# A hybrid layer of gated delta-rule attention and a feed-forward block: output products in other PSUM banks, one product for both heads' sums of squares, and a new order of the steps

## The chip, the cores and the metric

One Trainium2 chip, one of its cores. The time is device microseconds of one launch, the median of the runs. The kernel is float32 throughout; TensorE does a float32 product in two passes, so every product shows as two instructions in the trace.

## What is computed

```python
xn = layernorm(x)                                  # x: 4 batches x 256 tokens x 256
q, k, v, z = split(xn @ w_qkvz.T)                  # 32 heads, 64 wide each
q, k, v = causal_conv(q, k, v, width 4)
q = q / sqrt(sum(q*q) + eps) / 8;  k = k / sqrt(sum(k*k) + eps)
g, beta = -exp(A_log)*softplus(a + dt_bias), sigmoid(b)
for t in range(256):                               # per batch and head, state S is 64x64
    S = S * exp(g_t);  S = S + k_t * ((v_t - k_t.S) * beta_t);  o_t = q_t.S
o = o / sqrt(mean(o*o) + eps) * norm_weight * sigmoid(z)
attention = o @ w_out.T
ffn = hadamard(silu(h @ W_gate.T) * (h @ W_up.T)) @ W_down.T    # h = hadamard(xn), with scales
result = x + attention + ffn
```

## The kernel before

The recursion is done in chunks of 64 tokens: four chunks a sequence, 16 units (4 batches x 4 chunks) for each head. Inside a chunk it is a triangular system, whose inverse is built from 16x16 diagonal blocks; only the state goes from chunk to chunk. Two heads are one pair: head 0 on partitions 0 to 63, head 1 on 64 to 127, and 16 pairs are run one after the other as a software pipeline. One slice of 128 of the feed-forward block's 2 x 1024 rows goes with each pair. Work that stands ahead of the pairs (layer norm, transposes, gates, Hadamard factors) is in `setup`, and is the same in both kernels.

The steps of one pair, by the names that the code uses:
- `proj.0` to `proj.7`: projections of k, k, q, q, v, v, z, z, each 128x512 in one of two PSUM banks (`ring`). ACT does the first tap of the convolution out of the bank (or the tanh for z), DVE three more taps, each an instruction of its own that waits for the last. `ff`: gate and up products, into both `ring` banks.
- `ktr`, `vtr`: transposes of k and v into bank `TR`. `e`: a scan over decay rows, which gives a decay matrix. `stats`: the sums of squares of k and five small operations. `qsq`: q's sums of squares by products with a column of ones; ACT squares q first.
- `gram.0` to `gram.3`: k by k and q by k for one batch each, in the one bank `GR`; DVE multiplies each into `ATP`.
- `bout`, `bin`: SP writes the diagonal blocks to HBM (8 DMAs) and reads them back with another layout. `inv.0` to `inv.2`: DVE inverts all blocks at once, in 17 dependent instructions; ACT makes a transposed copy. `uout`, `uin`: out to HBM, and back in 16 small DMAs.
- `hz.j.H`: four rounds (j) for two halves of the units (H) that make the inverse of the 64x64 system from that of its blocks, products in bank `M[H]`, DVE's subtraction after each round.
- `delta.c`, `state.c`, `ks.c`, `o.t`: the recursion over chunks c in bank `CH`, outputs in bank `Z` for two halves t. `norm.t`: sum of squares of o (ACT, DVE), power -1/2 (POOL). `gated.t`: DVE scales. `turn.t`: transposes, and DVE's product with the z gate.
- `out.0` to `out.3`: the output products (two banks of 256 tokens for each half t), with the feed-forward block's down products in the two of the half `t == m % 2`; DVE adds each to the result `yacc`.

Each engine has its own written-out order, a string that `program` runs once per iteration. The letter before a step says which pair it is for: M this iteration's, A the next, P two ahead, L the one before, K two before. Each engine's iteration may start at another point of the pair's life, so the same letter on two engines need not be the same time. Every engine executes its list strictly in order, and a step first waits for its semaphores. SP's list holds the DMA steps.

Before, one iteration of TensorE is the end of the last pair's recursion and its outputs, then the next pair's first projections between the `hz` rounds, the grams and the start of the recursion:

```python
"""L.state.1 L.o.0 L.ks.2 M.proj.6 L.delta.2 M.vtr.1 L.state.2 M.proj.7 L.ks.3 L.turn.0 L.delta.3 L.o.1 M.ff M.qsq
L.turn.1 L.out.0 L.out.1 L.out.2 L.out.3 A.proj.0 M.hz.0.0 A.proj.1 A.proj.2 A.ktr.0 A.proj.3 M.hz.0.1 M.hz.1.0 A.ktr.1
M.hz.1.1 A.proj.4 M.hz.2.0 M.hz.2.1 A.gram.0 M.hz.3.0 M.hz.3.1 A.gram.1 M.delta.0 A.proj.5 M.state.0 A.gram.2 M.ks.1
A.gram.3 M.delta.1 A.vtr.0"""
```

Of the kernel before, what the change touches and what calls it, by code (L numbers as in the profile page):

```python
# [12 lines left out]
P = 128  # L13
# [5 lines left out]
C = 64  # L19
# [289 lines left out]
def pairs(nc, sem, sb, bank, k, xnT, beta, yacc, xh, wdf, coef, wqkvz, conv, wout, nw, wgu, drows, dblk, dub):  # L309

    with ExitStack() as ctx:
# [60 lines left out]
        TR, GR, M, CH, Z = bank[2], bank[3], [bank[4], bank[5]], bank[6], bank[7]  # L372
        hs = (slice(0, C), slice(C, P))
# [37 lines left out]
        with nc.Block() as block:  # L411
            @block.sync
            def _(sp):
# [78 lines left out]
                program({"load": load, "rload": rload, "fload": fload, "wload": wload, "oload": oload, "bout": bout, "bin": bin_, "uout": uout, "uin": uin}, """A.wload A.uout P.load A.uin A.oload P.rload P.bout P.fload P.bin""")  # L492

            @block.tensor
            def _(pe):
                def proj(m, q, i):

                    if i == 0:
                        pe.wait_ge(w_in, (m + 1) * 16)
                        wait(pe, acc_done, (m - 1) * 4 - 1)  # L500
                        wait(pe, hf_done, m)
                    if i == 1:
                        wait(pe, acc_done, (m - 1) * 4)
                    if i >= 2:
# [115 lines left out]
                def o(m, q, t):  # L620
# [3 lines left out]
                    wait(pe, on_done, m * 2 + t)  # L624
# [22 lines left out]
                def out(m, q, f):  # L647

                    t, j = f // 2, f % 2
                    if f == 0:  # L650
                        pe.wait_ge(wo_done, m + 1)
                        pe.wait_ge(hf_done, min(m + 2, PAIRS))
# [6 lines left out]
                    for b in (2 * j, 2 * j + 1):  # L659
                        dst = ring[j][:, (b % 2) * HID:(b % 2) * HID + HID]  # L660
                        last = nc.tensor.matmul(dst, oT[:, t, b, :], wo[:, q, :], start=True, stop=t != q)  # L661
                        if t == q:
# [4 lines left out]
                         "state": state, "o": o, "turn": turn, "out": out}, """L.state.1 L.o.0 L.ks.2 M.proj.6 L.delta.2 M.vtr.1 L.state.2 M.proj.7 L.ks.3 L.turn.0 L.delta.3 L.o.1 M.ff M.qsq  # L667
                         L.turn.1 L.out.0 L.out.1 L.out.2 L.out.3 A.proj.0 M.hz.0.0 A.proj.1 A.proj.2 A.ktr.0 A.proj.3 M.hz.0.1 M.hz.1.0 A.ktr.1
                         M.hz.1.1 A.proj.4 M.hz.2.0 M.hz.2.1 A.gram.0 M.hz.3.0 M.hz.3.1 A.gram.1 M.delta.0 A.proj.5 M.state.0 A.gram.2 M.ks.1
                         A.gram.3 M.delta.1 A.vtr.0""")  # L670

            @block.scalar
            def _(act):
# [56 lines left out]
                def oload(m, q):  # L730
# [7 lines left out]
                program({"proj": proj, "ff": ff, "dec": dec_, "ktr": ktr, "qsq": qsq, "inv": inv, "delta": delta, "norm": norm, "oload": oload}, """L.proj.6 K.delta.2 L.proj.7 K.delta.3 K.norm.1 L.inv.2 L.qsq L.ff M.proj.0 M.proj.1 M.proj.2 M.proj.3 M.ktr.0 M.ktr.1  # L738
                         M.proj.4 L.delta.0 L.oload M.dec M.proj.5 L.delta.1 L.norm.0""")

            @block.gpsimd
            def _(pool):
# [46 lines left out]
                program({"root": root, "gb": gb, "kd": kd_p, "kqg": kqg_p, "sd": sd, "norm": norm}, """P.gb.0 P.root P.gb.1 P.kd.0 A.sd.1 P.kqg.0 P.kd.1 P.kqg.1 A.sd.2 A.norm.0 A.norm.1""")  # L789

            @block.vector
            def _(dve):
# [135 lines left out]
                def norm(m, q, t):  # L928
# [4 lines left out]
                    if t == 0:  # L933
                        dve.wait_ge(qs_done, m + 1)
# [8 lines left out]
                def turn(m, q, t):  # L943
# [67 lines left out]
```

## Time and profile before

| | |
|---|---|
| time, median of 3 runs | 1015.8 us (1012.44 to 1017.12) |
| the profiled execution | 1015.0 us, span of its instructions 1013.0 us |
| mean granted TensorE clock | 0.957 of full |
| busy: TensorE / DVE / POOL / ACT | 88% / 70% / 26% / 21% |
| chain that ended last, by engine | TensorE 41%, DVE 26%, SP's queue 11%, DMA 10% |
| moved by DMA | 50.93 MB, 47 GB/s of HBM traffic |

The span is from the first to the last instruction. PE stands for TensorE's products, PEld for its weight loads. Busy time of PE is that of overlapping records whose ends are modelled, so the distance between the starts of two groups says more of what one costs. An entry in brackets behind a row of the timeline is idle time of that engine before the row, and what ended it.

### The profile page before, as it was taken

What the parts mean: (1) busy time and instruction counts of PE and PEld (TensorE: products, weight loads), DVE (VectorE), ACT (ScalarE), POOL (GpSimd) and SP (SyncE); (2) the same over time, 40 slices, a digit from 0 to 9 for tenths busy, and PEclk for the clock granted to TensorE, in tenths of its full rate; (3) what the DMA queues carried; (4) which work ended last, traced back from release to release, by engine and by line L of the source; (5) the groups of instructions that cost most, each with busy time, mean ns of one, the idle gap of its engine ahead of it and who ended that gap; (6) DMA issues with size and microseconds to landing.
All of it is one profiled execution on the core that took longest, in us unless ns stands there. A gap on an engine that the chain in (4) does not pass through costs nothing.

```text
span 1013.0 us, 33317 instructions
## 1 busy us (share of the span) xinstructions
PE 895.4 (88%) x14762; PEld 654.0 (65%) x14762; DVE 707.7 (70%) x1272; ACT 213.7 (21%) x384; POOL 262.6 (26%) x186
## 2 busy tenths in 40 slices
PE   1547599999999999999999999999999999999975
PEld 1324376676767676766767676767766676867664
DVE  5755486877777676867777676867777776768622
ACT  1211122222222121222222222222222221212200
POOL 0014051230505050422405050513314050503210
PEclk9879699999999999999999999999999999999978
DMA  4021302122041303032121403031221304031101
GB/s 167 11 63 27 89 6 62 38 63 57 12 91 29 90 8 79 21 66 52 44 59 29 91 12 91 7 72 43 49 55 34 85 13 90 15 83 25 31 10 42
DMA packets 133855, 50.93 MB, mean 50 GB/s; under 512 B 114768, under 2 KB 125264, under 8 KB 133584
## 3 DMA queue, kind: packets, MB, share of 16 engines
q1 hardware_dynamic: 133712, 48.81, 21.1%
q8 instruction: 116, 1.90, 0.8%
q14 instruction: 27, 0.22, 0.1%
HBM read 39.98 MB, written 7.60 MB: 47 GB/s over the span
## 4 chain that ended last, share of the span: by engine, by line
PE 41%; DVE 26%; SPq 11%; DMA 10%; issue 4%; ACT 3%; POOL 0%; POOLq 0%; DVEq 0%; ACTq 0%
PE bank L507 12%; DVE kq L798 8%; PE bank L582 8%; PE bank L563 6%; SPq L461 5%; PE bank L661 4%; DVE E L815 3%; DMA NT<-base_blocks 3%; SPq L485 3%; SPq L487 2%; DVE ATP L843 2%; DMA base_blocks<-ATP 2%; PE bank L580 2%; DMA X<-inverse_blocks 2%; DMA inverse_blocks<-UU 2%
## 5 line engine op out<-in xcount | busy, mean ns | idle before, releaser
L507 PE MATMUL bank<-xnT,wq 128*128 128x512 f32 x512 | 255.0, 624 | 21.8 <-DMA wq<-wqkvz_dram 16.8
L798 DVE SCALAR_TENSOR_TENSOR kq<-bank,cw,kq 128x510 f32<-128x510 f32 (+2 forms) x288 | 214.6, 745 | 58.4 <-ACT kq L685 50.4
L507 PEld LDWEIGHTS bank<-xnT,wq 128*128 128x128 f32 x512 | 89.7, 193 | 105.0 <-issue 68.0
L755 POOL TENSOR_TENSOR gb<-E,stat 128x512 f32<-128x512 f32 x32 | 33.3, 1042 | 447.2 <-issue 428.3
L685 ACT ACTIVATE kq<-bank,cw 128x512 f32<-128x512 f32 x96 | 66.0, 687 | 329.1 <-PE bank L507 329.1
L783 POOL TENSOR_TENSOR ost<-ost,cst 128x8 f32<-128x8 f32 x32 | 52.3, 1634 | 187.2 <-DVE ost L935 187.2
L954 DVE TENSOR_TENSOR yacc<-yacc,bank 128x512 f32<-128x512 f32 x64 | 44.0, 687 | 58.8 <-PE bank L663 40.3
L661 PE MATMUL bank<-wo,oT 128*128 128x256 f32 x256 | 82.0, 442 | 1.7 <-issue 1.6
L563 PE MATMUL bank<-kq 64*64 64x128 f32 x1024 | 69.3, 275 | 10.1 <-DVE ATP L843 10.1
L526 PEld LDWEIGHTS bank<-cst,kq 64*64 64x64 f32 x2048 | 65.9, 135 | 16.6 <-DVE kq L798 13.9
L773 POOL TENSOR_TENSOR kqg<-kq,rows 128x1024 f32<-128x1024 f32 x32 | 75.3, 2354 | 0.0
L526 PE MATMUL bank<-cst,kq 64*64 64x64 f32 x2048 | 72.4, 219 | 2.8 <-ACT ksqj L706 1.8
L843 DVE TENSOR_TENSOR ATP<-bank,gb 128x512 f32<-128x512 f32 x64 | 44.3, 692 | 40.5 <-PE bank L563 38.6
L582 PEld LDWEIGHTS bank<-X,Q 64*64 64x64 f32 x2048 | 62.9, 135 | 11.5 <-DVE X L911 11.4
L563 PEld LDWEIGHTS bank<-kq 64*64 64x64 f32 x1024 | 55.8, 135 | 13.7 <-issue 12.2
L582 PE MATMUL bank<-X,Q 64*64 64x16 f32 (+1 forms) x2048 | 64.6, 212 | 0.0
L661 PEld LDWEIGHTS bank<-wo,oT 128*128 128x128 f32 x256 | 54.3, 221 | 15.0 <-issue 3.8
L723 ACT ACTIVATE d<-bank 128x256 f32<-128x256 f32 x64 | 24.5, 383 | 186.5 <-PE bank L606 186.1
L630 PE MATMUL bank<-d,ATP 64*64 64x64 f32 x1024 | 56.7, 222 | 7.7 <-ACT d L723 7.7
L517 PE MATMUL bank<-xh,wguT 128*128 128x512 f32 x128 | 59.2, 605 | 1.3 <-DMA fc<-coef 1.3
L580 PEld LDWEIGHTS bank<-T,ATP 64*64 64x64 f32 x1024 | 34.1, 141 | 38.9 <-DMA X<-inverse_blocks 26.8
L630 PEld LDWEIGHTS bank<-d,ATP 64*64 64x64 f32 x1024 | 52.7, 135 | 9.9 <-ACT d L723 9.9
(130 smaller groups left out, 1330.8 us busy)
## 6 DMA issues: line engine op xcount, KB each, us to landing
rows<-decay_rows SPq DMA_DIRECT2D x64, 256.0 KB, 4.5
wq<-wqkvz_dram SPq DMA_DIRECT2D x16, 512.0 KB, 3.8
inverse_blocks<-UU SPq DMA_DIRECT2D x16, 256.0 KB, 2.2
base_blocks<-ATP SPq DMA_DIRECT2D x128, 16.0 KB, 1.7
wguT<-wgu_dram SPq DMA_DIRECT2D x8, 256.0 KB, 2.7
NT<-base_blocks SPq DMA_DIRECT2D x16, 128.0 KB, 2.5
U<-inverse_blocks SPq DMA_DIRECT2D x128, 16.0 KB, 2.0
woraw<-wout_dram SPq DMA_DIRECT2D x16, 128.0 KB, 2.3
```

The source lines that it names most:

```text
L507: last = nc.tensor.matmul(ring[i % 2][:], wq[:, q, kc, i // 2, :], xnT[:, kc, (i % 2) * 512:(i % 2) * 512 + 512], start=kc == 0, stop=kc = ...
L517: last = nc.tensor.matmul(ring[j][:], wguT[:, j, kc, :], xh[:, kc].rearrange("p (b t c) -> p b t c", b=B, t=2)[:, :, q, :], start=kc == 0, ...
L526: last = nc.tensor.matmul(TR[hs[h], u * C:u * C + C], kq[hs[h], which, b, w * C:w * C + C], k("eye")[hs[h]], start=True, stop=True)
L563: last = nc.tensor.matmul(GR[hs[h], w * P:w * P + P], kq[hs[h], 0, b, w * C:w * C + C], kq[hs[h], 0:2, b, w * C:w * C + C], start=True, st ...
L580: last = nc.tensor.matmul(dst, ATP[hs[h], q, u, 0, :], T16[hs[h], u, 0:n], start=True, stop=True)
L582: last = nc.tensor.matmul(dst, Q[hs[h], u, :], (U16[hs[h], u, C - n:C] if j == 1 else X[hs[h], q, u, C - n:C]), start=True, stop=True)
L630: last = nc.tensor.matmul(dst, ATP[hs[h], q, u, 1, :], d[hs[h], c % 2, b, :], start=True, stop=c == 0)
L661: last = nc.tensor.matmul(dst, oT[:, t, b, :], wo[:, q, :], start=True, stop=t != q)
L685: nc.scalar.activation(kq[:, i // 2, 2 * (i % 2):2 * (i % 2) + 2, :], split(ring[i % 2][:], 2), ACT.Copy, scale=cw[:, q, i // 2, 3:4]).the ...
L773: nc.gpsimd.tensor_tensor(kqg[:, q, :, half(H)].rearrange("p k u c -> p k (u c)"), src, g, ALU.mult).then_inc(kqg_done, 1)
L798: nc.vector.scalar_tensor_tensor(out=y[:, :, t:S], in0=p[:, :, 0:S - t], scalar=cw[:, q, i // 2, 3 - t:4 - t], in1=y[:, :, t:S], op0=ALU.m ...
L843: nc.vector.tensor_tensor(ATP[:, q, us], GR[:].rearrange("p (u k c) -> p u k c", u=NCH, k=2), gb_[:, us].unsqueeze(2).broadcast_to([P, NCH ...
```

## The change

Three things are changed, in the one function `pairs`.

Banks: the output products go to the banks of the `hz` rounds, `M[1 - j]`, in place of the projections' `ring`. `turn.0` stays in `M[0]`, `turn.1` goes to `Z`, where the recursion's outputs were. The waits follow the banks: the next pair's projections no longer wait for `acc_done` (DVE's additions), the first `hz` round does; `turn.1` no longer waits for `turn.0`'s use; `o.0` waits for the last pair's `turn.1`.

Sums of squares: `qsq` makes one product per unit with all 128 rows and two columns of ones (`hsel`), one column for each head, in place of two products with 64 rows and one column. The result stands on 64 partitions with the heads side by side, so DVE takes it in two reads.

Order: every engine's list is new, and SP's. Pair m's projections now belong to the iteration two before its outputs in all lists.

```diff
+        T2 = [M[0], Z]
@@ SP
-                program({...}, """A.wload A.uout P.load A.uin A.oload P.rload P.bout P.fload P.bin""")
+                program({...}, """K.oload M.load K.uin L.wload L.bout M.fload L.bin M.rload L.uout""")
@@ TensorE: proj
                     if i == 0:
                         pe.wait_ge(w_in, (m + 1) * 16)
-                        wait(pe, acc_done, (m - 1) * 4 - 1)
                         wait(pe, hf_done, m)
-                    if i == 1:
-                        wait(pe, acc_done, (m - 1) * 4)
@@ ktr
-                        wait(pe, qs_done, m)
+                        wait(pe, qs_done, m * 2)
@@ qsq
                     for u in range(UNITS):
-                        for h in range(2):
-                            last = nc.tensor.matmul(TR[hs[h], u:u + 1], kq[hs[h], 1, u // NCH, u % NCH * C:u % NCH * C + C], k("hsel")[hs[h], h:h + 1],
-                                                    start=True, stop=True)
+                        last = nc.tensor.matmul(TR[0:C, 2 * u:2 * u + 2], kq[:, 1, u // NCH, u % NCH * C:u % NCH * C + C], k("hsel"), start=True, stop=True)
@@ hz, j == 0
-                        wait(pe, ogT_done, m * 2)
+                        wait(pe, acc_done, m * 4 - H)
@@ o
-                    wait(pe, on_done, m * 2 + t)
+                    if t:
+                        pe.wait_ge(on_done, m * 2 + t)
+                    else:
+                        wait(pe, ogT_done, m * 2)
@@ turn
-                    if t:
-                        pe.wait_ge(ogT_done, m * 2 + 1)
-                    else:
-                        pe.wait_ge(hz_done, m * 8 + 8)
+                    pe.wait_ge(hz_done, m * 8 + 8)
-                            last = nc.tensor.matmul(M[0][hs[h], i * C:i * C + C], og[hs[h], i, :], k("eye")[hs[h]], start=True, stop=True)
+                            last = nc.tensor.matmul(T2[t][hs[h], i * C:i * C + C], og[hs[h], i, :], k("eye")[hs[h]], start=True, stop=True)
@@ out
-                        pe.wait_ge(hf_done, min(m + 2, PAIRS))
+                        pe.wait_ge(hf_done, m + 1)
-                        dst = ring[j][:, (b % 2) * HID:(b % 2) * HID + HID]
+                        dst = M[1 - j][:, (b % 2) * HID:(b % 2) * HID + HID]
@@ TensorE's order
-    (as quoted above)
+    """M.hz.0.1 M.hz.1.0 M.hz.1.1 A.gram.2 M.hz.2.0 M.hz.2.1 A.gram.3 M.hz.3.0 M.hz.3.1 P.proj.0 M.delta.0 A.vtr.1 M.state.0
+    P.proj.1 M.ks.1 A.qsq M.delta.1 P.proj.2 M.state.1 M.o.0 M.ks.2 P.proj.3 M.delta.2 P.ktr.0 M.state.2 P.proj.4 P.ktr.1
+    M.ks.3 P.gram.0 M.delta.3 M.turn.0 M.o.1 P.proj.5 M.out.0 M.out.1 P.proj.6 M.turn.1 P.vtr.0 P.proj.7 M.out.2 M.out.3
+    P.ff A.hz.0.0 P.gram.1"""
@@ ACT's order
-    """L.proj.6 K.delta.2 L.proj.7 K.delta.3 K.norm.1 L.inv.2 L.qsq L.ff M.proj.0 M.proj.1 M.proj.2 M.proj.3 M.ktr.0 M.ktr.1
-    M.proj.4 L.delta.0 L.oload M.dec M.proj.5 L.delta.1 L.norm.0"""
+    """A.proj.5 M.inv.2 A.ktr.1 A.proj.6 A.proj.7 A.ff A.qsq P.proj.0 M.delta.0 P.proj.1 M.delta.1 A.dec P.proj.2 P.proj.3
+    M.norm.0 M.delta.2 P.ktr.0 M.oload M.delta.3 M.norm.1 P.proj.4"""
@@ POOL's order
-    """P.gb.0 P.root P.gb.1 P.kd.0 A.sd.1 P.kqg.0 P.kd.1 P.kqg.1 A.sd.2 A.norm.0 A.norm.1"""
+    """K.sd.1 K.sd.2 K.norm.0 K.norm.1 M.kqg.0 M.kqg.1 M.gb.0 M.kd.0 M.gb.1 M.root M.kd.1"""
@@ DVE: qsq, norm, turn, out
-                    nc.vector.tensor_scalar(qs[:, q], TR[:, 0:UNITS], EPS, EPS * D, ALU.add, ALU.mult).then_inc(qs_done, 1)
+                    for h in range(2):
+                        nc.vector.tensor_scalar(qs[hs[h], q], TR[0:C, h:2 * UNITS:2], EPS, EPS * D, ALU.add, ALU.mult).then_inc(qs_done, 1)
-                        dve.wait_ge(qs_done, m + 1)
+                        dve.wait_ge(qs_done, m * 2 + 2)
-                    ... in1=split(M[0][:], B) ...
+                    ... in1=split(T2[t][:], B) ...
-                    nc.vector.tensor_tensor(y, y, split(ring[j][:], 2), ALU.add).then_inc(acc_done, 1)
+                    nc.vector.tensor_tensor(y, y, split(M[1 - j][:], 2), ALU.add).then_inc(acc_done, 1)
@@ DVE's order
-    """A.stats M.hz.2.0 M.hz.2.1 A.gram.0 M.hz.3.0 M.hz.3.1 A.gram.1 A.proj.4 M.state.0 A.gram.2 M.ks.1 A.gram.3 A.proj.5
-    M.state.1 M.norm.0 M.ks.2 A.vtr.0 M.gated.0 A.vtr.1 M.state.2 A.inv.0 M.ks.3 A.inv.1 A.inv.2 M.norm.1 M.turn.0
-    M.gated.1 A.ff A.qsq M.turn.1 M.out.0 M.out.1 M.out.2 M.out.3 P.proj.0 A.hz.0.0 P.proj.1 P.proj.2 P.e A.hz.0.1 P.proj.3
-    A.hz.1.0 A.hz.1.1"""
+    """L.out.3 A.gram.0 M.hz.0.0 A.gram.1 M.hz.0.1 M.hz.1.0 A.vtr.0 M.hz.1.1 A.gram.2 M.hz.2.0 A.ff M.hz.2.1 A.gram.3 M.hz.3.0
+    M.hz.3.1 P.proj.0 M.state.0 A.vtr.1 M.ks.1 P.proj.1 A.inv.0 M.state.1 A.qsq P.proj.2 M.ks.2 A.inv.1 M.norm.0 M.state.2
+    P.proj.3 M.ks.3 M.gated.0 A.inv.2 M.turn.0 M.norm.1 P.proj.4 M.gated.1 P.proj.5 M.turn.1 M.out.0 M.out.1 P.e P.stats
+    M.out.2"""
```

## Rows read from the trace of the kernel before

**Rows 1.** The page, busy time of TensorE: busy us (share of the span), instructions.
```profile
PE 895.4 (88%) x14762; PEld 654.0 (65%) x14762; DVE 707.7 (70%) x1272; ACT 213.7 (21%) x384; POOL 262.6 (26%) x186
```

**Rows 2.** Windows of two periods: start:end, length, busy (instructions), clock, DMA, GB/s.
```profile
core 0: us, PE busy (x) PEld busy (x) DVE busy (x) ACT busy (x) POOL busy (x), PEclk, DMA share, GB/s
499.80:555.50 55.70, 52.93 (x915) 38.84 (x912) 41.71 (x77) 12.78 (x23) 15.99 (x11) 1.00 0.24 54
555.50:611.70 56.20, 54.46 (x915) 40.02 (x912) 41.83 (x77) 12.77 (x23) 15.99 (x11) 0.97 0.22 47
```

**Rows 3.** Timeline of TensorE over one period: start, us, what [idle before].
```profile
499.81 3.70 PE L517 MATMUL bank<-xh,wguT 128*128 128x512 f32 x8
503.74 2.03 PE L553 MATMUL bank<-cst,kq 64*64 64x1 f32 x64 [0.23 <-ACT kq L711]
505.63 1.13 PE L644 MATMUL bank<-cst,og 64*64 64x64 f32 x32
506.91 0.67 PE L661 MATMUL bank<-wo,oT 128*128 128x256 f32 x2 [0.15 <-issue]
...
515.07 1.13 PE L580 MATMUL bank<-T,ATP 64*64 64x48 f32 x32 [0.83 <-DMA X<-inverse_blocks]
...
521.24 1.98 PE L507 MATMUL bank<-xnT,wq 128*128 128x512 f32 x4 [0.33 <-DVE kq L798]
...
535.43 1.99 PE L507 MATMUL bank<-xnT,wq 128*128 128x512 f32 x4
537.35 0.68 PE L617 MATMUL bank<-d,kd 64*64 64x64 f32 x16
...
539.79 1.09 PE L563 MATMUL bank<-kq 64*64 64x128 f32 x16 [0.42 <-DVE ATP L843]
...
544.34 0.68 PE L592 MATMUL bank<-St,kqg 64*64 64x64 f32 x16 [0.18 <-DVE St L926]
...
553.46 0.34 PE L630 MATMUL bank<-d,ATP 64*64 64x64 f32 x4 [0.48 <-ACT d L723]
```

**Rows 4.** Timeline of TensorE's weight loads in the setup.
```profile
24.88 3.83 PEld L289 LDWEIGHTS bank<-wbas,xnT 128*64 128x64 f32 x128 [1.04 <-DVE xnT L177]
```

**Rows 5.** Windows around one fall of the clock, and of `hz.2` to `delta.0`.
```profile
447.00:450.40 3.40, 3.16 (x96) 2.80 (x96) 2.25 (x4) 1.12 (x2) 1.56 (x1) 1.00 0.81 240
450.50:453.90 3.40, 3.25 (x13) 2.54 (x9) 1.55 (x4) 0.00 (x0) 0.00 (x0) 0.50 0.36 34
...
529.30:535.40 6.10, 6.10 (x177) 6.02 (x176) 4.34 (x12) 0.69 (x1) 3.85 (x2) 1.00 0.01 3
```

**Rows 6.** Timeline of ACT and DVE: transposed inverse, `e`, last gram, taps, `inv.0`.
```profile
502.10 0.64 ACT L717 ACTIVATE UU<-UU 128x256 f32<-128x256 f32 x1 [1.59 <-DVE UU L897]
...
523.57 2.29 DVE L815 TENSOR_TENSOR_SCAN E<-rows,cst 128x1024 f32<-128x1024 f32 x1
...
540.92 0.69 DVE L843 TENSOR_TENSOR ATP<-bank,gb 128x512 f32<-128x512 f32 x1 [0.95 <-PE bank L563]
541.53 2.30 DVE L798 SCALAR_TENSOR_TENSOR kq<-bank,cw,kq 128x510 f32<-128x510 f32 x3
...
550.39 0.42 DVE L874 TENSOR_TENSOR UU<-NT,cst 128x256 f32<-128x256 f32 x1 [0.84 <-DMA NT<-base_blocks]
```

**Rows 7.** Timeline at the fill and at the tail, TensorE and DVE.
```profile
61.86 5.13 PE L507 MATMUL bank<-xnT,wq 128*128 128x512 f32 x8 [16.82 <-DMA wq<-wqkvz_dram]
...
89.73 0.69 DVE L843 TENSOR_TENSOR ATP<-bank,gb 128x512 f32<-128x512 f32 x1 [1.27 <-PE bank L563]
...
119.29 0.99 PE L580 MATMUL bank<-T,ATP 64*64 64x48 f32 x14 [4.62 <-DMA X<-inverse_blocks]
...
965.27 3.16 PE L580 MATMUL bank<-T,ATP 64*64 64x48 f32 x64 [2.34 <-DMA X<-inverse_blocks]
...
997.06 1.97 PE L644 MATMUL bank<-cst,og 64*64 64x64 f32 x32 [4.05 <-DVE og L941]
```

**Rows 8.** The page's groups: count, busy us, mean ns of one, idle before.
```profile
L685 ACT ACTIVATE kq<-bank,cw 128x512 f32<-128x512 f32 x96 | 66.0, 687 | 329.1 <-PE bank L507 329.1
L783 POOL TENSOR_TENSOR ost<-ost,cst 128x8 f32<-128x8 f32 x32 | 52.3, 1634 | 187.2 <-DVE ost L935 187.2
```

More of the change, by code:

```diff
@@ L491, in _ @@
                     sp.dma_start(nwh[hs[h], :], nw).then_inc(nw_in, 16)
-                program({"load": load, "rload": rload, "fload": fload, "wload": wload, "oload": oload, "bout": bout, "bin": bin_, "uout": uout, "uin": uin}, """A.wload A.uout P.load A.uin A.oload P.rload P.bout P.fload P.bin""")
+                program({"load": load, "rload": rload, "fload": fload, "wload": wload, "oload": oload, "bout": bout, "bin": bin_, "uout": uout, "uin": uin}, """K.oload M.load K.uin L.wload L.bout M.fload L.bin M.rload L.uout""")
             @block.tensor
@@ L666, in _ @@
                 program({"proj": proj, "ff": ff, "ktr": ktr, "vtr": vtr, "qsq": qsq, "gram": gram, "hz": hz, "ks": ks, "delta": delta,
[L667 to L670, printed above, removed]
+                         "state": state, "o": o, "turn": turn, "out": out}, """M.hz.0.1 M.hz.1.0 M.hz.1.1 A.gram.2 M.hz.2.0 M.hz.2.1 A.gram.3 M.hz.3.0 M.hz.3.1 P.proj.0 M.delta.0 A.vtr.1 M.state.0
+                         P.proj.1 M.ks.1 A.qsq M.delta.1 P.proj.2 M.state.1 M.o.0 M.ks.2 P.proj.3 M.delta.2 P.ktr.0 M.state.2 P.proj.4 P.ktr.1
+                         M.ks.3 P.gram.0 M.delta.3 M.turn.0 M.o.1 P.proj.5 M.out.0 M.out.1 P.proj.6 M.turn.1 P.vtr.0 P.proj.7 M.out.2 M.out.3
+                         P.ff A.hz.0.0 P.gram.1""")
             @block.scalar
@@ L737, in _ @@
                 act.wait_ge(nwh_done, 1)
-                program({"proj": proj, "ff": ff, "dec": dec_, "ktr": ktr, "qsq": qsq, "inv": inv, "delta": delta, "norm": norm, "oload": oload}, """L.proj.6 K.delta.2 L.proj.7 K.delta.3 K.norm.1 L.inv.2 L.qsq L.ff M.proj.0 M.proj.1 M.proj.2 M.proj.3 M.ktr.0 M.ktr.1
-                         M.proj.4 L.delta.0 L.oload M.dec M.proj.5 L.delta.1 L.norm.0""")
+                program({"proj": proj, "ff": ff, "dec": dec_, "ktr": ktr, "qsq": qsq, "inv": inv, "delta": delta, "norm": norm, "oload": oload}, """A.proj.5 M.inv.2 A.ktr.1 A.proj.6 A.proj.7 A.ff A.qsq P.proj.0 M.delta.0 P.proj.1 M.delta.1 A.dec P.proj.2 P.proj.3
+                         M.norm.0 M.delta.2 P.ktr.0 M.oload M.delta.3 M.norm.1 P.proj.4""")
             @block.gpsimd
@@ L788, in _ @@
                 nc.gpsimd.memset(Q[:], 0.0).then_inc(preset, 1)
-                program({"root": root, "gb": gb, "kd": kd_p, "kqg": kqg_p, "sd": sd, "norm": norm}, """P.gb.0 P.root P.gb.1 P.kd.0 A.sd.1 P.kqg.0 P.kd.1 P.kqg.1 A.sd.2 A.norm.0 A.norm.1""")
+                program({"root": root, "gb": gb, "kd": kd_p, "kqg": kqg_p, "sd": sd, "norm": norm}, """K.sd.1 K.sd.2 K.norm.0 K.norm.1 M.kqg.0 M.kqg.1 M.gb.0 M.kd.0 M.gb.1 M.root M.kd.1""")
             @block.vector
@@ L946, in turn @@
                     wait(dve, op_ready, (m - 1) * 4 + 2 * t + 2)
-                    nc.vector.scalar_tensor_tensor(out=oT[:, t], in0=zt[:, q, :, t * P:t * P + P], scalar=1.0, in1=split(M[0][:], B),
+                    nc.vector.scalar_tensor_tensor(out=oT[:, t], in0=zt[:, q, :, t * P:t * P + P], scalar=1.0, in1=split(T2[t][:], B),
                                                    op0=ALU.add, op1=ALU.mult).then_inc(ogT_done, 1)
@@ L953, in out @@
                     y = yacc[:].rearrange("p (b t) m -> p b t m", t=2)[:, 2 * j:2 * j + 2, t, :]
-                    nc.vector.tensor_tensor(y, y, split(ring[j][:], 2), ALU.add).then_inc(acc_done, 1)
+                    nc.vector.tensor_tensor(y, y, split(M[1 - j][:], 2), ALU.add).then_inc(acc_done, 1)
                 program({"proj": proj, "ff": ff, "e": e, "stats": stats, "gram": gram, "vtr": vtr, "qsq": qsq, "inv": inv, "hz": hz, "ks": ks,
-                         "state": state, "norm": norm, "gated": gated, "turn": turn, "out": out}, """A.stats M.hz.2.0 M.hz.2.1 A.gram.0 M.hz.3.0 M.hz.3.1 A.gram.1 A.proj.4 M.state.0 A.gram.2 M.ks.1 A.gram.3 A.proj.5
-                         M.state.1 M.norm.0 M.ks.2 A.vtr.0 M.gated.0 A.vtr.1 M.state.2 A.inv.0 M.ks.3 A.inv.1 A.inv.2 M.norm.1 M.turn.0
-                         M.gated.1 A.ff A.qsq M.turn.1 M.out.0 M.out.1 M.out.2 M.out.3 P.proj.0 A.hz.0.0 P.proj.1 P.proj.2 P.e A.hz.0.1 P.proj.3
-                         A.hz.1.0 A.hz.1.1""")
+                         "state": state, "norm": norm, "gated": gated, "turn": turn, "out": out}, """L.out.3 A.gram.0 M.hz.0.0 A.gram.1 M.hz.0.1 M.hz.1.0 A.vtr.0 M.hz.1.1 A.gram.2 M.hz.2.0 A.ff M.hz.2.1 A.gram.3 M.hz.3.0
+                         M.hz.3.1 P.proj.0 M.state.0 A.vtr.1 M.ks.1 P.proj.1 A.inv.0 M.state.1 A.qsq P.proj.2 M.ks.2 A.inv.1 M.norm.0 M.state.2
+                         P.proj.3 M.ks.3 M.gated.0 A.inv.2 M.turn.0 M.norm.1 P.proj.4 M.gated.1 P.proj.5 M.turn.1 M.out.0 M.out.1 P.e P.stats
+                         M.out.2""")
                 dve.wait_ge(acc_done, PAIRS * 4)
```

## The prediction

> **What bounds the kernel now.** I read the page's busy table first: TensorE is busy 88% of the span, far ahead of the rest [rows 1]. That is an average over fill, steady part and tail, so next came the windows of two neighbouring periods, each from one pair's `ff` to the next one's. They last 55.70 and 56.20 us; DVE is busy 41.8 us, ACT 12.8 and POOL 16.0 in either, so only TensorE is near full [rows 2]. The first `hz.0.0` of a pair stands at 119.29 us for pair 0 and at 965.27 for pair 15: 15 periods of 56.4 us, 846 of the 1013 us [rows 7]. The reader is to see that this is a kernel of one period, repeated.
>
> Then the order of TensorE's work in the 55.70 us window, looking for idle time in brackets. Seven rows have it: 0.23 before `qsq` (ACT's squares), 0.15 before `out.0`, 0.83 before `hz.0.0` (the inverse arriving by DMA), 0.33 before a projection (DVE's taps), 0.42 before `gram.3` (the one gram bank), 0.18 and 0.48 in the recursion [rows 3]. They sum to 2.62 us, which leaves 53.1 us of issued products. In the second window the granted clock is 0.97 for a whole period [rows 2]. Short windows show why: 3.4 us at 0.50 while the first output products run, right after `qsq` and `turn.1` [rows 5]. Such a stretch comes in 8 of the 14 periods between pair 1's `ff` and pair 15's and costs half its length, 1.7 us, so about 1.0 us per period. 53.1 + 2.6 + 1.0 is 56.7 against 56.4 measured: the period is accounted for. TensorE's order and its stalls set the time, not another engine.
>
> **q's sums of squares.** Before, 64 instructions (one product is two passes) take 503.74 to 505.63, 1.89 us, 29.5 ns each, two halves of the array side by side. After there are 32, each with 128 rows, 64 weight columns and two moving columns. Nearest row: in the setup, 128 weight loads of just this shape (128x64) take 3.83 us, 29.9 ns each [rows 4]. So 32 take 0.95 us, and 0.94 us per period goes. At the other end a full-height product costs as much as the two half-height ones beside each other (59 ns) and the saving is nothing. I take 0.94, since the row has the same weights; both ends stay. The Trainium skill (TensorE: Matmul & The Clock Gate, LDWEIGHTS) says that a weight load takes its number of columns over 1.2 GHz, whatever the rows: 53 ns for 64 columns, 1.7 us for 32, a saving of 0.2 us. The trace's 29.9 ns disagrees with it; by the page the sum below would be some 11 us longer. DVE's second small read (0.17 us more) lies in DVE's idle time, 14 us a period.
>
> **Banks.** The output products leave `ring`; so the next projections wait for no `acc_done`, and `ff` needn't be consumed before `out.0`. In exchange `hz.j.H` waits for DVE to have added `out.2` and `out.3`. `turn.0` writes `M[0]`, `turn.1` writes `Z`, so neither waits for the other. These cost no work; they are worth what the order makes of them.
>
> **The order.** I followed one period through the five queues with the rows' durations: projection 1.91 us [rows 3], its tap on ACT 0.69, three taps on DVE 2.33, `E` 2.29, DVE's small pieces 0.3 to 0.7 [rows 6, 8], POOL's power 1.63 [rows 8], a group of 32 small products 0.95, 0.2 us for it to drain, 0.04 from one engine to the next. Let T be the end of `o.1`.
> - From T TensorE has `proj.5`, `out.0`, `out.1`, `proj.6`, `turn.1`, `vtr.0`, `proj.7`, `out.2`, `out.3`, `ff`: 16.7 us. Inside it the norm (ACT 0.6, DVE 0.9, POOL 1.65, DVE 0.7) has DVE's taps of `proj.4` beside it and is ready at T+4.9, before `turn.1` at T+6.2 to 7.3. `proj.6` waits for `proj.4`'s taps (T+4.3): no wait where `out.0` and `out.1` carry the feed-forward products (1.73 us each), 0.55 us where they don't (0.87 each). Per period 0.3.
> - DVE meanwhile does `turn.1`, `out.0`, `out.1`, `E`, `stats` (2.1), `out.2`, `out.3`, done at T+15.8. `hz.0.0` is at T+16.7: it doesn't wait for the bank, with 0.9 us to spare.
> - The inverse: ACT's transposed copy stands behind `proj.5`'s tap and starts at T+2.7. Copy, DMA out, 16 DMA issues and landing took from 502.10 to 515.07, 13.0 us [rows 3, 6]; `oload`, now ahead of the load on SP, adds 0.2. T+15.9, 0.8 us ahead of need. The 0.83 us wait of now is hidden.
> - `hz` and `gram` alternate for 10.3 us, with 8 to 9 us of DVE work. `hz.1.1` has 0.15 us to spare, `hz.3.1` 0.4. `vtr.0` on DVE waits for POOL's root, done 3.2 us into the stretch and needed at 4.5.
> - `bout` starts after `gram.3`; `inv.0` can start 9.5 us after that eviction (540.92 to 550.39 now [rows 6]). Its place on DVE comes 10.7 us after it, as two projections' taps stand between. SP's `fload` and `rload` lie in DMA time that nothing waits for.
> - In the recursion `delta.2`'s copy stands behind `proj.3`'s tap and `norm.0` on ACT; `state.2` waits 0.35 us for it. Every other step finds its inputs ready, by 0.1 to 1 us.
>
> So the new period is 53.1 - 0.94 + 0.35 + 0.3 = 52.8. The clock should not fall as now, since `qsq` stands between heavier steps and is half as long.
>
> **The sum.** The fill gets longer: now pair 0's last gram is evicted at 89.73 and `hz.0.0` follows at 119.29. After, all eight projections, `ff` and POOL's root come before that eviction; it ends near 95.5. Inverse blocks +9.5, inversion 12 (it shares DVE with pair 1's taps), copy and DMAs 13: `hz.0.0` near 131. Then 14 full periods, 739, to 870. The period that leads to pair 15's `hz.0.0` has no projections: 9 to the last eviction, 9.5, inversion 11.6, 13.0: 43.5, to 913.5. The tail is now 47.7 us (965.27 to 1013.0); in it `turn.1` waits idle for 4.05 us for the norm [rows 7], and now `out.0` and `out.1` lie in that wait: 44. Span 957.5; the profiled run was 2 us above its span and the median 0.8 above it: 960. With some 2 us for a handoff that I misjudged, **962 us**, 5.3% less.
>
> **Rivals.**
> 1. The full-height product is no cheaper than the pair: +0.94 x 15 = 14 us, **976**. For it: half-height pairs do run side by side. Against: [rows 4].
> 2. The new order has slips of its own. Six handoffs have under 1 us to spare, the old order lost 2.6 us per period in seven. If the new one loses 2.6 instead of 0.6, +2.0 x 15: **991**.
> 3. The change doesn't do what it says: a loop through DVE and the DMAs (inverse late, then `hz`, then `out.3`) takes the idle time's place, 3.5 us per period; the period stays at 56.3 and the time at **1013**. Against it: DVE has 14 us idle, and the chain to `inv.0` has 1.2 us to spare.
> 4. Slower: the clock. The new order puts 10.3 us of 64-row products with 16 to 48 columns together, without a projection. If TensorE ran at 1.2 instead of 2.4 GHz for all of it, each period is 10.3 us longer, **1115**. It decides from 3.5 us per period on, 7 us at half clock; one stretch of 3.4 us per period gives only +1.7 x 15, 987. For it: the clock fell with TensorE busy 3.16 of the last 3.40 us [rows 5]. Against: `hz.2` to `gram.1` are 6.1 us of the same products, at 1.00 [rows 5]. The same page of the Trainium skill (Part 1) has the gate follow how busy TensorE has been, at half or full rate; both levels are in the rows, but the profile's busy time does not foretell the fall, so the page settles nothing here.
>
> **Chances.** Forecast 0.60; rival 1 0.08; rival 2 0.17; rival 3 0.05; rival 4 0.03; 0.07 that the fill, the tail or the handoffs come out better, below 950. The range leaves out rivals 3 and 4, the upper part of rival 2 and the lower part of the last case: 946 to 990. Within 0.5% is about what a measurement of this kernel can't tell from no change. Faster 0.92, same 0.04, slower 0.04.
>
> **What would show it.** Steady distance between `hz.0.0` of neighbouring pairs near 52.8 us. L553's successor: 32 instructions a pair, 0.95 us. No fall of the clock behind it. Idle before the first `hz` product near nothing; 0.35 us before `state.2`; up to 0.55 before `proj.6` in every second pair. First `hz.0.0` near 131, the last near 913. I am wrong if waits on DVE's `X` or `Q`, on `yacc`, or on the inverse's DMA come to over 1 us a period, or if the clock reads 0.50 in the `hz` stretch.

## The result, and the profile after

The changed kernel takes 975.3 us (median of 4 runs, 972.64 to 977.65) against 1014.5 us of the kernel before (median of 4, the three known before and one more): ratio 0.961, with 95% interval 0.957 to 0.965. It is faster by 3.9%; 5.3% was forecast, and the time lies inside the range of 946 to 990.

The page of the kernel after: busy time, and the chain that ended last.

```profile
PE 883.1 (91%) x14250; PEld 652.2 (67%) x14250; DVE 707.4 (73%) x1288; ACT 209.5 (22%) x384; POOL 264.3 (27%) x186
...
PE 77%; DVE 10%; issue 2%; SPq 2%; DMA 1%; POOL 1%; ACT 1%; POOLq 0%; DVEq 0%; ACTq 0%
```

512 instructions fewer on TensorE (16 units x 2 for each of 16 pairs), and the chain is now TensorE for 77% of the span, where it was 41%, with DVE, SP's queue and the DMAs in between. That is what filling the waits looks like.

Two neighbouring periods, from one pair's first `hz.0.0` to the next one's, and a window inside the first, right after the sums of squares (columns as in [rows 2]):

```profile
400.55:454.62 54.07, 53.53 (x881) 39.46 (x880) 41.67 (x78) 12.49 (x23) 17.76 (x14) 0.97 0.23 49
454.62:506.29 51.67, 51.67 (x881) 38.87 (x880) 41.33 (x77) 12.49 (x23) 14.32 (x10) 1.00 0.27 59
420.20:423.20 3.00, 3.00 (x12) 0.98 (x12) 0.96 (x6) 0.52 (x3) 0.00 (x0) 0.55 0.49 122
```

Busy 51.67 of 51.67 us: in every second period TensorE shows no gap at all. The other kind is 2.4 us longer and has the clock at 0.97. From pair 0's `hz.0.0` (137.17) to pair 14's (877.69) it is 14 periods of 52.9 us, 52.8 having been forecast.

The timeline of TensorE in the longer period, at the sums of squares (L550) and at `proj.6` (441.90):

```profile
417.19 2.03 PE L550 MATMUL bank<-cst,kq 128*64 128x2 f32 x32
419.15 0.68 PE L602 MATMUL bank<-Y,X 64*64 64x64 f32 x16
419.76 3.06 PE L505 MATMUL bank<-xnT,wq 128*128 128x512 f32 x4
422.75 1.12 PE L613 MATMUL bank<-d,kd 64*64 64x64 f32 x16
...
441.90 1.98 PE L505 MATMUL bank<-xnT,wq 128*128 128x512 f32 x4 [0.54 <-DVE kq L794]
```

The wait of 0.54 us before `proj.6`, in every second pair, is the one that was forecast at 0.55. But the 32 merged products take 1.96 us (417.19 to 419.15), 61 ns each, about as long as the 64 of before (1.89 us). And the clock falls behind them: the next projection takes 2.99 us in place of 1.91. There are 7 such falls in the steady part, one every second period (209, 315, 420, 526, 632, 738, 844 us), where the kernel before had 8.

### The profile page after: what moved, and what is told of

Its sections match the earlier page's. It is cut to its first block, busy times and chain, and to the rows that moved or that the text cites. A ratio compares the mean times of both kernels' runs of the same rounds, so it can differ in the third digit from the quotient of the medians.

```text
span 970.6 us, 32338 instructions
## 1 busy us (share of the span) xinstructions
PE 883.1 (91%) x14250; PEld 652.2 (67%) x14250; DVE 707.4 (73%) x1288; ACT 209.5 (22%) x384; POOL 264.3 (27%) x186
## 3 DMA queue, kind: packets, MB, share of 16 engines
q8 instruction: 112, 1.84, 0.8%
## 4 chain that ended last, share of the span: by engine, by line
PE 77%; DVE 10%; issue 2%; SPq 2%; DMA 1%; POOL 1%; ACT 1%; POOLq 0%; DVEq 0%; ACTq 0%
PE bank L505 23%; PE bank L578 9%; PE bank L524 6%; PE bank L515 5%; PE bank L559 5%; PE bank L657 4%; PE bank L576 3%; PE bank L602 3%; PE bank L550 3%; DVE kq L794 3%; PE bank L613 3%; PE bank L629 3%; PE bank L588 3%; PE bank L659 3%; PE bank L640 2%
## 5 line engine op out<-in xcount | busy, mean ns | idle before, releaser
L505 PE MATMUL bank<-xnT,wq 128*128 128x512 f32 x512 | 266.5, 646 | 30.3 <-DMA wq<-wqkvz_dram 16.8
L794 DVE SCALAR_TENSOR_TENSOR kq<-bank,cw,kq 128x510 f32<-128x510 f32 (+2 forms) x288 | 214.6, 745 | 58.7 <-ACT kq L681 51.3
L775 POOL TENSOR_TENSOR Sd<-St,dec 128x256 f32<-128x256 f32 x32 | 19.9, 620 | 300.2 <-DVE St L920 195.7
L524 PEld LDWEIGHTS bank<-cst,kq 64*64 64x64 f32 x2048 | 65.5, 136 | 17.6 <-DVE kq L794 13.8
L657 PE MATMUL bank<-wo,oT 128*128 128x256 f32 x256 | 70.2, 387 | 2.9 <-DVE yacc L951 1.5
L657 PEld LDWEIGHTS bank<-wo,oT 128*128 128x128 f32 x256 | 49.3, 194 | 22.1 <-issue 13.3
L629 PE MATMUL bank<-d,ATP 64*64 64x64 f32 x1024 | 59.7, 231 | 0.0
L629 PEld LDWEIGHTS bank<-d,ATP 64*64 64x64 f32 x1024 | 57.0, 144 | 0.0
L908 DVE TENSOR_TENSOR X<-U,bank 128x384 f32<-128x384 f32 (+2 forms) x96 | 40.1, 418 | 22.6 <-PE bank L578 22.6
L631 PE MATMUL bank<-St,kqg 64*64 64x64 f32 x768 | 54.4, 224 | 0.0
```

Source lines behind the costliest of these rows:

```text
L524: last = nc.tensor.matmul(TR[hs[h], u * C:u * C + C], kq[hs[h], which, b, w * C:w * C + C], k("eye")[hs[h]], start=True, stop=True)
L629: last = nc.tensor.matmul(dst, ATP[hs[h], q, u, 1, :], d[hs[h], c % 2, b, :], start=True, stop=c == 0)
L631: last = nc.tensor.matmul(dst, kqg[hs[h], q, 1, u, :], St[hs[h], c % 2, b, :], start=False, stop=True)
L794: nc.vector.scalar_tensor_tensor(out=y[:, :, t:S], in0=p[:, :, 0:S - t], scalar=cw[:, q, i // 2, 3 - t:4 - t], in1=y[:, :, t:S], op0=ALU.m ...
```

## The experiments

All ratios are to the kernel before, run on the same chip in turn. "Falls" are stretches of 3.4 us with the clock at 0.50, counted from 150 us to the `hz.0.0` of pair 14; the mean period is that of the 14 up to there. Both come from the one profiled execution of each kernel. All falls stand behind the sums of squares, but for two of the four in the row "outputs behind `turn.1`".

| kernel | time, us | ratio to before (95%) | falls | mean period |
|---|---|---|---|---|
| changed | 975.3 | 0.961 (0.957 to 0.965) | 7 | 52.9 |
| merged squares alone, old order | 1013.0 | 0.996 (0.994 to 0.999) | 7 | 56.5 |
| banks alone, old order | 1015.5 | 0.998 (0.996 to 1.000) | 6 | 56.2 |
| new order and banks, old squares | 963.8 | 0.948 (0.945 to 0.951) | 1 | 52.1 |
| changed, squares with 32 columns | 960.8 | 0.945 (0.942 to 0.948) | 0 | 52.2 |
| changed, outputs behind `turn.1` | 999.2 | 0.983 (0.980 to 0.986) | 4 | 55.0 |
| changed, squares in alternate halves | 948.8 | 0.933 (0.930 to 0.936) | 0 | 51.4 |
| changed, late `kqg` | 970.3 | 0.954 (0.951 to 0.957) | 7 | 53.0 |
| old squares, late `kqg` | 961.9 | 0.943 (0.940 to 0.946) | 4 | 52.5 |
| alternate halves, late `kqg` | **946.1** | 0.930 (0.927 to 0.932) | 0 | 51.3 |
| that, `ktr.1` before `proj.6` | 953.0 | 0.935 (0.933 to 0.938) | 0 | 51.9 |

**Merged squares alone.** The diff's `qsq` and DVE's two reads, put into the kernel before.

> The kernel before with one part of the change alone: q's sums of squares by one full-height product per unit, and DVE's two reads; banks and order as before. Theory 1 (a full-height product whose result goes to 64 partitions costs as much as the two half-height ones side by side): the step still takes 1.9 to 2.0 us, the clock still falls behind it, the time is that of before, 1014 us within 3. Rival (the product costs 29.9 ns as the setup's weight loads, and something in the new order made it slow): the step takes 0.95 us and the time is 995 to 1002 us.

1013.0 us. The timeline of TensorE:

```profile
450.78 2.03 PE L552 MATMUL bank<-cst,kq 128*64 128x2 f32 x32 [0.23 <-ACT kq L709]
452.73 1.15 PE L642 MATMUL bank<-cst,og 64*64 64x64 f32 x32
```

1.95 us for 32 instructions in the old order too, for 1.89 of before. Theory 1 holds: the merge saves no time on TensorE. Why the whole is 0.4% shorter, with an interval that just leaves out 1, no run shows.

**The old squares in the new order.**

```diff
-                        last = nc.tensor.matmul(TR[0:C, 2 * u:2 * u + 2], kq[:, 1, ...], k("hsel"), ...)
+                        for h in range(2):
+                            last = nc.tensor.matmul(TR[hs[h], u:u + 1], kq[hs[h], 1, ...], k("hsel")[hs[h], h:h + 1], ...)
```

> The changed kernel with the old two half-height products per unit and DVE's one read; new banks and new order. Theory 1: the step takes 1.9 us, the time stays at 975 us within 3, so all of the gain is the order and the banks. Rival (merging is worth something that the step's own length does not show, such as fewer instructions in TensorE's queue): 980 to 990 us.

963.8 us: faster than the changed kernel, which neither expectation had. The step takes 1.84 us, but the clock falls once, at 418 us, and only the period with that fall is 53.9 us long. So order and banks together bring 5.2%, and the merge takes 1.3 points of it back. Six falls fewer at 1.6 us, and a step shorter by 0.12 us in 16 pairs, are 11.5 us of estimate, and the times differ by 11.5. The falls vary between executions, though: one of the six took 969.5 us, at a mean clock of 0.952 for 0.959 to 0.962 in the others.

**Alternate halves.**

```diff
-                        last = nc.tensor.matmul(TR[0:C, 2 * u:2 * u + 2], kq[:, 1, ...], k("hsel"), ...)
+                        last = nc.tensor.matmul(TR[hs[u % 2], u // 2 * 2:u // 2 * 2 + 2], kq[:, 1, ...], k("hsel"), ...)
...
                     for h in range(2):
+                        for r in range(2):
+                            nc.vector.tensor_scalar(qs[hs[h], q, r:UNITS:2], TR[hs[r], h:UNITS:2], EPS, EPS * D, ALU.add, ALU.mult).then_inc(qs_done, 1)
```

> The changed kernel with the full-height products of even units written to PSUM partitions 0 to 63 and those of odd units to 64 to 127, and DVE's reads four in place of two; the same values. Theory 1 says that neighbouring products run side by side when they go to different halves of the partitions, as those of the setup do: the step takes 0.95 to 1.0 us in place of 1.96, and the clock no longer falls behind it; period 51.7 and 54.1 become about 50.7 and 51.3, the time 945 to 952 us. Rival (the setup's 29.9 ns come from its other shape, 32 moving columns from another tile): the step stays at 1.96 us, the time at 975.

948.8 us, in the range. The timeline of TensorE, and the windows of two periods:

```profile
460.26 1.10 PE L550 MATMUL bank<-cst,kq 128*64 128x2 f32 x32
461.29 0.68 PE L602 MATMUL bank<-Y,X 64*64 64x64 f32 x16
```

```profile
391.77:443.62 51.85, 50.94 (x880) 37.79 (x881) 41.75 (x79) 11.94 (x23) 16.76 (x12) 1.00 0.23 51
443.62:494.43 50.81, 50.60 (x880) 37.87 (x880) 41.66 (x79) 12.39 (x23) 14.11 (x10) 1.00 0.27 60
```

The longer of the two is usually 51.63 us. The same instructions on the same operands take 1.03 us where they took 1.96; only the half of the partitions that the result goes to has changed, and with it DVE's reads, four for two. The setup's products, from which the forecast took 29.9 ns, alternate between the halves too, after every four instructions (`bank[4][h * C:h * C + C]`). The Trainium skill says as much (TensorE: Matmul & The Clock Gate, Part 3: small products run concurrently when their outputs lie in different column groups, which the output's start partition picks); this pair of runs agrees. With the shorter period the inverse has become nearly the limit: before four of the fourteen steady `hz.0.0` it lands only 0.04 us ahead, once after a wait of 1.18 us.

```profile
391.77 1.14 PE L576 MATMUL bank<-T,ATP 64*64 64x48 f32 x32 [1.18 <-DMA X<-inverse_blocks]
```

**32 columns.** The second operand is `hsel` and the 30 constants behind it: more work in the array, the same number of products.

```diff
-                        last = nc.tensor.matmul(TR[0:C, 2 * u:2 * u + 2], kq[:, 1, ...], k("hsel"), ...)
+                        last = nc.tensor.matmul(TR[0:C, 32 * u:32 * u + 32], kq[:, 1, ...], k("hsel32"), ...)
...
-                        nc.vector.tensor_scalar(qs[hs[h], q], TR[0:C, h:2 * UNITS:2], ...)
+                        nc.vector.tensor_scalar(qs[hs[h], q], TR[0:C, h:32 * UNITS:32], ...)
```

> The changed kernel with 32 moving columns in place of 2 in each product of the sums of squares; the first two are the columns of ones, the other 30 results are read by nobody. Theory 3 (every second period is 2.4 us longer mostly because the clock falls after the sums of squares, whose products use the array little): the step still takes about 2 us, the clock stays at 1.00 in the steady part, the longer periods go from 54.1 to about 52.3, the time is 960 to 965 us. Rival (the longer periods come from handoffs that differ between even and odd pairs): 975 us or more.

960.8 us, in the range; its windows and the step:

```profile
400.81:453.32 52.51, 51.97 (x881) 38.80 (x881) 41.43 (x77) 11.90 (x23) 17.07 (x13) 1.00 0.23 51
453.32:505.02 51.70, 51.70 (x882) 38.88 (x881) 41.35 (x77) 12.51 (x23) 14.34 (x10) 1.00 0.27 59
```

```profile
417.45 2.05 PE L551 MATMUL bank<-cst,kq 128*64 128x32 f32 x32
419.44 0.68 PE L603 MATMUL bank<-Y,X 64*64 64x64 f32 x16
```

Sixteen times the columns in 1.99 us in place of 1.96, and no fall. The longer period goes from 54.07 to 52.51; the 0.8 us left over the shorter one are the wait before `proj.6` and what goes with it. Theory 3 holds: without the falls the 14 periods take 731.2 us in place of 740.5. That is 9.3 us; the medians differ by 14.5, and where the rest comes from the traces don't say (this one is of the slowest of six executions, the changed kernel's of the fastest of four). All six executions have a mean clock of 0.965 to 0.969, all four of the changed kernel 0.948 to 0.954, so the falls aren't missing by chance.

**Banks alone.** All of the diff's lines on banks and waits, none on squares and order.

> The kernel before with the new banks and their waits alone; squares and order as before. Theory 2 (the banks pay nothing by themselves, they only allow the new order): 1014 us within 4, the waits for DVE's taps, the gram bank, the inverse and ACT's copies all still there. Rival (the waits on acc_done and hf_done were a hidden part of the period): up to 1.4 us per period less, 993 to 1000 us.

1015.5 us: theory 2, no gain by itself. The waits of [rows 3] are still there. The one for the gram bank (us in all, times, longest us) is the same 10.1 us in both kernels:

```profile
PE bank L561 <- DVE ATP L841: 10.1, 17, 2.8
```

**Outputs behind turn.1.**

```diff
-P.proj.5 M.out.0 M.out.1 P.proj.6 M.turn.1 P.vtr.0
+P.proj.5 P.proj.6 M.turn.1 M.out.0 M.out.1 P.vtr.0
```

> The changed kernel with the first two output products moved in TensorE's list from between proj.5 and proj.6 to behind turn.1; all else as changed. Theory 4 (the new order pays because work that is ready stands in front of each wait, here the output products in front of the taps of proj.4): proj.6 waits 2.4 us in every period in place of 0.54 in every second one, 2.1 us more per period, 1005 to 1009 us. Rival (the queue is bound by issued work alone, and such a wait is made up elsewhere in the period): 975 us within 4.

999.2 us, 24 us more in place of 32. The wait came as computed, in every period:

```profile
456.43 1.98 PE L505 MATMUL bank<-xnT,wq 128*128 128x512 f32 x4 [2.27 <-DVE kq L794]
```

The mean period is 55.0 us, the 2.1 more than 52.9 that were forecast. The steady periods are 54.55 us, 2.9 more than 51.67 and 2.1 more than 52.48, the changed kernel's longer period without a fall (shown below). The clock fell only 4 times, all before 275 us, and not once in the eleven periods of 54.55 us. Two of the four (at 212.5 and 270.6 us) stand behind the sums of squares, the other two (178.4 and 236.4) behind the new wait itself:

```profile
233.00:236.40 3.40, 1.38 (x3) 0.68 (x4) 3.26 (x6) 1.97 (x4) 3.40 (x2) 1.00 0.47 127
236.40:239.80 3.40, 3.40 (x35) 2.28 (x34) 1.82 (x3) 0.00 (x0) 2.69 (x2) 0.50 0.58 160
```

That the time rose by 24 and not by 32 us is not in these periods: they took 29.6 us more, while the last period and the tail are 3.1 us shorter in the profiled executions. Theory 4 holds.

**Late kqg.** Twice: on the alternate halves, and on the changed kernel.

```diff
-K.sd.1 K.sd.2 K.norm.0 K.norm.1 M.kqg.0 M.kqg.1 M.gb.0 M.kd.0 M.gb.1 M.root M.kd.1
+K.sd.1 K.sd.2 K.norm.0 K.norm.1 M.gb.0 M.kd.0 M.gb.1 M.root M.kd.1 M.kqg.0 M.kqg.1
```

> The kernel with alternate halves (948.8 us), with POOL's two long products kqg moved in its list from ahead of gb to behind the last kd. Theory 5 (in the fill, two of DVE's inversion steps take 2.0 and 1.3 us more while a kqg runs on POOL, and that delays the first hz round): no DVE inversion step over 1.1 us, first hz.0.0 3 us earlier, steady period as before, 944 to 947 us. Rival (the fill waits for something else, or kqg now delays hz or the squares in every period): 949 us or more.

> The changed kernel with POOL's kqg moved behind the last kd and nothing else; squares merged as changed. Theory 5: first hz.0.0 3 us earlier, about 971 us. For the clock: if merged products in this order draw it down in themselves, 7 or so falls again in the steady part and periods of 51.7 and 54.1 in turn; if the falls were the luck of where the period fell, a fill that is 3 us shorter gives another number, down to 1 as with the two half-height products, and 961 us.

946.1 and 970.3 us. The reason to try it is in the changed kernel's fill, where DVE and POOL stand so:

```profile
111.79 2.61 DVE L881 TENSOR_TENSOR prod<-UU 128x64 f32<-128x64 f32 x2
119.99 2.39 DVE L893 TENSOR_TENSOR prod<-UU,part 128x512 f32<-128x512 f32 x1
...
427.38 0.56 DVE L881 TENSOR_TENSOR prod<-UU 128x64 f32<-128x64 f32 x2
436.30 1.09 DVE L893 TENSOR_TENSOR prod<-UU,part 128x512 f32<-128x512 f32 x1
```

```profile
111.89 2.38 POOL L769 TENSOR_TENSOR kqg<-kq,rows 128x1024 f32<-128x1024 f32 x1 [17.65 <-DVE kq L794]
118.25 3.19 POOL L769 TENSOR_TENSOR kqg<-kq,rows 128x1024 f32<-128x1024 f32 x1 [3.98 <-DVE kq L794]
```

With `kqg` elsewhere the two steps take their steady 0.57 and 1.08 us:

```profile
113.64 0.57 DVE L881 TENSOR_TENSOR prod<-UU 128x64 f32<-128x64 f32 x2
...
119.80 1.08 DVE L893 TENSOR_TENSOR prod<-UU,part 128x512 f32<-128x512 f32 x1
```

So the stretching is POOL's doing. It was worth less than I expected. The last piece of the inverse landed 1.4 us earlier in the changed kernel (134.16 for 135.60) and 2.9 on the halves (131.12 for 134.03), and the first `hz.0.0` came 1.4 us earlier (135.77 for 137.17) and 1.7 on the halves, not 3. In this fill `hz.0.0` waits last for something else: it follows `ff` without a gap, 1.6 us after the inverse has landed, and `ff` waits for ACT's tanh of `proj.7`. In the changed kernel:

```profile
133.57 3.67 PE L515 MATMUL bank<-xh,wguT 128*128 128x512 f32 x8 [0.78 <-ACT zt L685]
137.17 1.13 PE L576 MATMUL bank<-T,ATP 64*64 64x48 f32 x32
```

The gains in time are hardly clear of the noise. On the halves it is 2.7 us, and the intervals of the ratios overlap; on the changed kernel it is 5.0 us, with intervals that just don't, but the two profiled spans differ by only 1.3 us. The other half of the question, the clock, came out as 7 falls again, but not at the same places. The first three stand in every second period, as before; then one came in the other kind, and the rest kept to that one. So the two kinds of period can be seen with and without a fall:

```profile
665.86:719.16 53.30, 53.30 (x881) 39.37 (x881) 40.99 (x77) 12.49 (x23) 13.96 (x10) 0.97 0.26 57
719.16:771.64 52.48, 51.94 (x882) 38.80 (x881) 41.95 (x78) 12.49 (x23) 18.13 (x14) 1.00 0.23 50
```

53.30 with a fall for 51.67 without, 54.08 for 52.48: a fall costs 1.6 us in either.

**The old squares with late kqg**, the diff of two runs above together.

> The changed kernel with the two half-height products per unit and POOL's kqg behind the last kd: the same as the one with late kqg that fell 7 times in the steady part, but for the squares. If the shape of the merged product draws the clock down in this order: at most 2 falls in the steady part, 957 to 961 us. Rival (the single fall with half-height products was luck): 5 or more falls, 967 to 971 us.

961.9 us and 4 falls: between the two expectations. Two shapes, two positions: merged 7 and 7, in pairs 1 and 4. The trace with 4 is that of the slowest of six executions (965.1 us). Over all of them the mean clock is 0.948 to 0.956 in the ten executions with merged products, 0.952 to 0.964 in the twelve with pairs. The pairs draw the clock down less often in this order, but not never, and by a number that varies.

**ktr.1 in front of the wait.** The idea was to win the 0.54 us before `proj.6` in the fastest kernel.

```diff
-P.proj.4 P.ktr.1 M.ks.3 ... M.out.0 M.out.1 P.proj.6 M.turn.1
+P.proj.4 M.ks.3 ... M.out.0 M.out.1 P.ktr.1 P.proj.6 M.turn.1
```

> The kernel with alternate halves and late kqg (946.1 us), with the transposes ktr.1 moved in TensorE's list from behind proj.4 to in front of proj.6, so that 0.95 us of ready work stands before the wait for proj.4's taps. Theory 4 (ready work in front of a wait pays its length, up to the wait): the periods of 51.63 and 50.81 us in turn become 50.8 to 51.0 in all, 939 to 942 us. Rival (ktr.1 was itself cover for ks.3, or its copies on ACT now hold up vtr.0 or the next projections): 946 us or more.

953.0 us, 7 us slower. Nearly all periods are now alike, but at 51.84, not 50.8. The wait before `proj.6` is gone; two others, before `delta.2` and `delta.3`, stand in every period. The first was there before, but only in every second one; the second is new:

```profile
420.02 0.68 PE L602 MATMUL bank<-Y,X 64*64 64x64 f32 x16 [0.21 <-DVE Y L914]
...
425.89 0.68 PE L602 MATMUL bank<-Y,X 64*64 64x64 f32 x16 [0.39 <-DVE Y L914]
```

`ktr.1` had stood in front of `ks.3` and `gram.0`. Without it TensorE comes to `delta.3` before DVE has made `Y`, which stands in DVE's list behind the taps of `proj.3`. The rival was right in number, and nearly in cause: the cover was for `delta.3`, two steps on. The kernel with alternate halves and late `kqg` stays the fastest: 7% under the one before, 3% under the changed one. A piece of ready work covers one wait or another; moving it paid for one and lost the other.

## Why the prediction was right, and where it was off

**The bound and the mechanism: right.** TensorE's order and its stalls set the time, and filling them was the gain. Banks alone bring nothing measurable, and moving one pair of outputs out of its place costs 2.1 to 2.9 us a period. That the order needs the banks is argued from the waits in the diff; no run had the new order with the old banks. Rivals 2, 3 and 4 did not come. The new order's own slips in the steady part were the 0.54 us of every second period and little else. The inverse was in time, though with less room than the 0.8 us forecast in some periods: it landed 0.04 to 1.2 us before `hz.0.0`, and at the short end was itself waited for (294.79, 612.13 us). The clock read 1.00 in the stretch of `hz` and `gram`:

```profile
457.40:464.80 7.40, 7.40 (x230) 7.39 (x226) 5.84 (x11) 1.06 (x1) 0.61 (x1) 1.00 0.01 3
```

**q's sums of squares: the term was mis-sized.** 0.94 us per period was taken off; the merged step took 1.96 us where it had been 1.89. The step that failed is the choice of the row: [rows 4] has the same weights but a result that alternates between the halves of the partitions, which the row doesn't show and the code does. Rival 1's premise was true. That its 976 us came within 1 us of the time is luck: its 14 us stand for a longer period, and the period was as forecast; 12 of the 13 us missing were outside the steady periods (below). The 53 ns of the Trainium skill's page (TensorE: Matmul & The Clock Gate, LDWEIGHTS) lay nearer to the 61 ns measured than the row did, but the load's own length is not what decides: in alternate halves the same 64-column loads follow every 32 ns.

**"The clock should not fall as now": wrong.** It fell 7 times in 14 periods, some 0.8 us per period. The reason given, heavier steps around a shorter one, had the length from the same row.

**The period came out right, 52.9 for 52.8, by luck: errors cancelled.** The two points above make the forecast 1.8 us too short. On the other side, the 53.1 us of "issued products" held waits that have no bracket. In the timeline before:

```profile
524.13 1.10 PE L582 MATMUL bank<-U,Q 64*64 64x48 f32 x32
525.07 1.15 PE L526 MATMUL bank<-cst,kq 64*64 64x64 f32 x32
526.37 1.13 PE L582 MATMUL bank<-U,Q 64*64 64x48 f32 x32
```

From the first start to the second it is 0.94 us for 32 small products, from the second to the third 1.30 for as many: 0.36 us of waiting for DVE's `Q` that the modelled end of the row before covers. The brackets of [rows 3] hide such pieces too. From `turn.1` to `out.0` it is 1.28 us (505.63 to 506.91), 1.13 without the bracket; after, `turn.1` takes 0.98 (497.21 to 498.19). The clean period of after is 51.67 us with the same products, so by this difference 1.5 us of the 53.1 were such waits, and the new order removed them too. The wait before `state.2`, forecast at 0.35, shows only as 0.14 us of that kind (`ktr.0` takes 1.09 us from start to start, for 0.95).

**The ends: 12 of the 13 us.** By the profiled span (970.6 against 957.5): the first `hz.0.0` at 137.2 for 131, 14 periods 740.5 for 739, the short period 45.1 for 43.5, the tail 47.8 for 44. In the fill the last gram was evicted at 95.9 and `inv.0` began at 105.9, as computed (95.5 and 105); then the inversion took 17 us, not 12, with POOL's `kqg` in two of its steps (3.3 us) and a wait for two projections in part at half clock (105.68, 5.40 us). The inverse landed at 135.6, for 130 by the forecast's terms, and `ff`, which the forecast did not have in this sum, held `hz.0.0` for the other 1.6 us. In the tail `out.0` and `out.1` did move into the wait, but what was left then ran mostly at half clock:

```profile
955.23 1.15 PE L640 MATMUL bank<-cst,og 64*64 64x64 f32 x32 [2.12 <-DVE og L938]
957.81 1.19 PE L657 MATMUL bank<-wo,oT 128*128 128x256 f32 x2 [1.43 <-DVE oT L944]
958.80 1.06 PE L659 MATMUL bank<-wfd,hf 128*128 128x256 f32 x2
```

These last two output products take 6.4 us (957.81 to 964.2) where 1.73 us each, 3.5 us, would do at full rate. From the end of `o.1` to the last addition it is 13.8 us, for 14.4 before, so 0.6 us of the 3.7 expected were won.

**What stays open** is why the merged squares pull the clock down more often than the pairs, 7 and 7 against 1 and 4. In the old order they don't (7 against 8). The length of the period alone is not the reason for the falls with 2 columns and their absence with 32: without a fall the two kinds of period are 51.67 and 52.48 us with 2, 51.70 and 52.51 with 32. But order or length does count: with the same merged products there were no falls in the eleven periods of 54.55 us. More varied periods with either shape would be needed.

## What to carry to other kernels

On a saturated in-order queue, take the gap-free period from distances between starts of like groups, not from the bracketed idle times: the rest is what an order can win. When a cost is borrowed from a row, check that the code behind it has the same neighbours: two products that write different halves of the partitions ran in the time of one. Each piece of ready work covers one wait; before moving it, price the wait that it covers now.

## What was unexpected of the hardware

- Full-height products with 64 weight columns: 61 ns each when all results go to partitions 0 to 63, 32 ns when they alternate with 64 to 127.
- 32 moving columns cost 1.99 us per 32 products, 2 columns 1.96 us, and the wide ones kept the clock up; adding unread work made the kernel 1.5% faster (960.8 for 975.3 us).
- DVE's products of two SBUF operands, 0.27 and 1.09 us alone, took up to 2.31 and 2.39 us beside POOL's `kqg`. Where DVE's product started first (118.21 us, for 1.02), it kept its time and the `kqg` of 118.25 took 3.19 us in place of 2.38. The Trainium skill (Perfetto Trace Analysis, Optimizing Scalar/DVE Operations) says that the two engines share an SBUF read port. The runs agree: moving `kqg` brought both back. DVE's taps, which read one operand from PSUM, were not stretched in the steady part (2.30 us beside `kqg`).
